# Feed-forward input transposed by VectorE and transfers instead of TensorE, for seven of twelve chunks

## The reference

```
x = x + attn_a(layernorm(x), Wq, bq, Wk, bk, Wv, bv, Wo, bo)     # 16 heads of 16, softmax over 512 keys
x = x + ffn(layernorm(x), W1, W2, W3)
x = x + attn_b(layernorm(x), Wv, Wg, bg, Wq, bq, Wo)             # sigmoid gates, decaying scan over the sequence
x = x + ffn(layernorm(x), W1, W2, W3)

def ffn(x, W1, W2, W3):          # D = 256, H = 1024
    hidden = silu(x @ W1.T) * (x @ W3.T)
    hidden = fwht(hidden)        # Walsh-Hadamard transform, folded into W2 here
    return hidden @ W2.T
```

## Time and profile before

| what | value |
|---|---|
| median of 3 runs | 574.08 us (574.04 to 577.14) |
| the profiled execution | 574.17 us, its span 572.4 us |
| busy share of TensorE, VectorE, ScalarE, GpSimd | 97%, 65%, 56%, 31% |
| moved by transfers | 25.74 MB in 17979 packets |

### The profile page before, as it was taken

How to read it: one execution, slowest core, us unless ns; L and a number is a source line. 1 busy time by engine, 2 the same in 40 slices (tenths; PEclk the granted TensorE clock), 3 DMA queues, 4 the chain that set the end, 5 groups by cost and what they waited for, 6 DMA issues and landing times.

```text
span 572.4 us, 8932 instructions
## 1 busy us (share of the span) xinstructions
PE 557.8 (97%) x3276; PEld 388.6 (68%) x3276; DVE 374.2 (65%) x715; ACT 319.7 (56%) x595; POOL 176.4 (31%) x209
## 2 busy tenths in 40 slices
PE   8999999999999988899999999999999999999997
PEld 4543433344334433378888888888888888988887
DVE  6998878888888899754363544747886336254433
ACT  3678888867876886833234242266775333434231
POOL 5796375552545333510101010223332010101000
PEclk9999999999999999999999999999999999999999
DMA  7357320330032020010000000000000010010101
GB/s 230 101 185 236 118 74 3 113 112 2 18 124 86 25 125 3 12 64 1 1 0 1 1 1 2 1 0 1 1 1 1 2 37 1 1 37 1 38 1 38
DMA packets 17979, 25.74 MB, mean 45 GB/s; under 512 B 3032, under 2 KB 11224, under 8 KB 17552
## 3 DMA queue, kind: packets, MB, share of 16 engines
q1 hardware_dynamic: 16716, 24.10, 13.0%
q10 hardware_dynamic: 1220, 1.07, 0.6%
HBM read 10.89 MB, written 5.24 MB: 28 GB/s over the span
## 4 chain that ended last, share of the span: by engine, by line
PE 89%; DVE 4%; ACT 3%; issue 2%; DMA 1%; ACTq 0%; POOL 0%; SPq 0%; DVEq 0%; POOLq 0%
PE PS L367 86%; DVE mxr L1077 3%; PE PS L378 2%; ACT qf L805 1%; ACT PR L912 1%; PE PS L585 1%; DMA X<-in_x 1%; DVE PR L1216 0%; DVE OT L1142 0%; DMA ring<-mT 0%; ACT XNs L974 0%; ACT XNs L965 0%; ACTq L874 0%; DVE X L1244 0%; ACT xf L789 0%
## 5 line engine op out<-in xcount | busy, mean ns | idle before, releaser
L367 PE MATMUL PS<-xTh,ring 128*128 128x512 f32 x608 | 188.7, 392 | 0.0
L1077 DVE TENSOR_REDUCE mxr<-PS 128x1 f32<-128x512 f32 x256 | 163.1, 682 | 26.4 <-PE PS L367 25.8
L912 ACT ACTIVATE PR<-PS 128x512 f32<-128x512 f32 x256 | 138.2, 604 | 35.9 <-PE PS L367 35.5
L367 PEld LDWEIGHTS PS<-xTh,ring 128*128 128x128 f32 x608 | 113.2, 188 | 23.6 <-issue 1.7
L367 PE MATMUL PS<-xTl,ring 128*128 128x512 f32 x304 | 110.1, 391 | 0.0
L367 PE MATMUL PS<-ring 50*128 50x512 f32 (+1 forms) x512 | 99.3, 450 | 5.0 <-DVE mxr L1077 3.8
L1216 DVE TENSOR_TENSOR PR<-PR,PS 128x512 f32<-128x512 f32 x64 | 43.8, 684 | 88.7 <-PE PS L367 66.4
L789 ACT ACTIVATE AOh<-PR 128x512 fp32r<-128x512 f32 x72 | 45.5, 632 | 95.5 <-DVE PR L1216 89.6
L367 PEld LDWEIGHTS PS<-ring 50*128 50x128 f32 (+1 forms) x512 | 41.3, 184 | 82.4 <-ACT PR L912 54.9
L1319 POOL TENSOR_TENSOR xTl<-xf,xTh 128x512 fp32r<-128x512 f32 x30 | 41.1, 1384 | 144.4 <-ACT xTh L789 144.4
L980 ACT ACTIVATE PR<-PS 128x512 f32<-128x512 f32 x64 | 38.0, 594 | 79.2 <-PE PS L367 79.2
(11 more groups left out here) (132 smaller groups left out, 635.1 us busy)
## 6 DMA issues: line engine op xcount, KB each, us to landing
ring<-qh SPq DMA_DIRECT2D x48, 128.0 KB, 2.7
ring<-ql SPq DMA_DIRECT2D x24, 128.0 KB, 2.7
ring<-weight_scratch SPq DMA_DIRECT2D x3, 1024.0 KB, 4.8
weight_scratch<-in_w SPq DMA_DIRECT2D x2, 1024.0 KB, 6.7
X<-in_x SPq DMA_DIRECT2D x3, 512.0 KB, 6.7
out<-X SPq DMA_DIRECT2D x6, 256.0 KB, 2.2
X<-in_w SPq DMA_DIRECT2D x1, 1024.0 KB, 5.4
ring<-AOh SPq DMA_DIRECT2D x8, 128.0 KB, 2.8
```

The costliest lines, as they stand in the source:

```text
L367: return nc.tensor.matmul(dst, lhsT, rhs, start=start, stop=stop, skip_group_check=True)
L912: nc.scalar.activation(PR[:, j % 8, :], PS[:, kq_bank(j), :], ACT.Exp, scale=HD ** -0.5)\
L1077: nc.vector.tensor_reduce(mxr[:, S % 2, blk, TT * p + t:TT * p + t + 1], PS[:, QK0 + i % 3, :], AX.X, ALU.max, negate=True).then_inc(max_d ...
```

## The change

For the seven preparations named above, TensorE's transposes and ScalarE's copies out of the banks go. In their place:

- `normalise` writes `XNs` in another order, (half of the features, token tile, feature), so that each half is a stretch of 512 columns. It comes after f = 1 and not after f = 3, and `prepare` after f = 0 and not f = 1.
- `turn_blocks`, after f = 2, VectorE: two `transpose` of 128 by 512 from `XNs` to `PR` slots 4 and 5. Each turns the 32 by 32 blocks in themselves; a block stays on its 32 partitions.
- `turned_blocks`, SP: 16 transfers, one for each pair of a source and a destination group of 32 partitions, from `PR` to `xf`. Each moves 32 partitions by 8 runs of 32 float32 values (128 bytes), 32 KB in 256 runs. SP waits for `lnT_ready` (the two transposes) and `x_lo` (`xf` free again) ahead of them.
- ScalarE: no `ln_evacuate`; `ln_hi` comes after f = 6 and not f = 5 and waits until all 16 transfers have landed (`xf_in`).
- In chunk 3, `centre` stays after f = 5, `scale` comes behind `ln_hi` after f = 6, and the two extra statistics come after f = 3 and f = 4.

```diff
+        def by_dim(v):
+            return v.rearrange("p t n -> p (t n)").rearrange("p (k t u) -> p k t u", k=KD, u=P)
+        def turned_block(a, c):
+            u = slice(32 * a, 32 * a + 32), slice(32 * c, 32 * c + 32)
+            return (xf[u[1], :, :].rearrange("p k (t u) -> p (k t) u", u=P)[:, :, u[0]],
+                    PR[u[0], 4:6, :].rearrange("p k (t u) -> p (k t) u", u=P)[:, :, u[1]])
...
+            def turned_blocks(L):
+                sp.wait_ge(lnT_ready, 2 * L + 2)
+                sp.wait_ge(x_lo, 2 * L)
+                for a in range(4):
+                    for c in range(4):
+                        sp.dma_start(*turned_block(a, c)).then_inc(xf_in, DMA)
             weights_in(W_MEM)
+            for n in range(BATCH):
+                turned_blocks(n + BATCH + 1)
...
+                if c < BATCH - 1:
+                    turned_blocks(3 * BATCH + 1 + c)
...
-                    if f == 4 and not last:
-                        pe.wait_ge(xns_ready, n + BATCH + 1)
-                        if n == 0:
-                            pe.wait_ge(x_done, 2 * BATCH)
-                        ln_transpose(0, PS[:, 6, :])
-                        ln_transpose(1, PS[:, 7, :])
...
-                    pe.wait_ge(x_f, 2 * (n + BATCH + 1))
+                    pe.wait_ge(x_f, 2 * (n + 1))
...
             def ln_hi(L, dt, par):
-                act.wait_ge(x_f, 2 * (L - 1) + dt + 1)
+                n = L - BATCH - 1
+                if n % (2 * BATCH) < BATCH and n >= 0:
+                    act.wait_ge(xf_in, 16 * DMA * (n + 1 - n // (2 * BATCH) * BATCH))
+                else:
+                    act.wait_ge(x_f, 2 * (L - 1) + dt + 1 - (2 * BATCH if n >= 0 else 0))
...
-                    if n == BATCH - 1 and f == 6:
-                        scale(1, 0)
-                    if f == 5 and not last:
+                    if n == BATCH - 1 and f == 5:
+                        centre(2 * BATCH + 1, 1, 0)
+                    if f == 6 and not last:
                         for dt in range(KD):
-                            ln_evacuate(n + BATCH + 1, dt, PS[:, 6 + dt, :])
                             ln_hi(n + BATCH + 1, dt, 1 - par)
                         if n == BATCH - 1:
-                            centre(2 * BATCH + 1, 1, 0)
+                            scale(1, 0)
...
+            def turn_blocks(L, i):
+                dve.wait_ge(xns_ready, L)
+                if i:
+                    dve.wait_ge(xf_in, 16 * DMA * i)
+                for dt in range(KD):
+                    nc.vector.transpose(PR[:, 4 + dt, :], by_dim(XNs[:, :, :])[:, dt, :, :].rearrange("p t u -> p (t u)"))\
+                        .then_inc(lnT_ready, 1)
...
-                    if f == 1 and not last and not prepared:
+                    if f == 0 and not last and not prepared:
                         dve.wait_ge(x_done, 2 * (n + BATCH) - 2 * (n == 0))
                         pause()
                         prepare(n, X0)
-                    if n == BATCH - 1 and f in (2, 4):
-                        pause()
-                        prepare(BATCH + f // 2 - 1, f // 2 * TT, f // 2 * TT)
-                    if f == 3 and not last:
+                    if f == 1 and not last:
                         dve.wait_ge(rstd_done, n + 6)
                         normalise(X0, X0 if prepared else 0, n + BATCH + 1)
+                    if f == 2 and not last:
+                        turn_blocks(n + BATCH + 1, n - n // (2 * BATCH) * BATCH)
+                    if n == BATCH - 1 and f in (3, 4):
+                        pause()
+                        prepare(BATCH + f - 3, (f - 2) * TT, (f - 2) * TT)
...
+            dve.wait_ge(xf_in, 16 * DMA * BATCH)
             for c in range(BATCH):
                 mem_chunk(BATCH + c, TT * c, TT * ((c + 3) % BATCH))
```

More of the change, by code:

```diff
@@ L145, in build @@
             sem(n) for n in ("swhi_done", "swlo_done", "rwhi_done", "rwlo_done", "stk_ready", "stk_tmp", "stk_done"))
+        xf_in = sem("xf_in")
         nmean_done, nmem_done, mem_centred = (sem(n) for n in ("nmean_done", "nmem_done", "mem_centred"))
@@ L1061, in normalise @@
             def normalise(X0, n0, L):
-                if L:
-                    dve.wait_ge(lnT_ready, 2 * L)
+                dve.wait_ge(lnT_ready, 2 * L)
                 for t in range(TT):
-                    last = normalise_tile(X0 + t, n0 + t, t)
+                    last = nc.vector.tensor_scalar(by_dim(XNs[:, :, :])[:, :, t, :],
+                                                   X[:, X0 + t, :].rearrange("p (k u) -> p k u", k=KD),
+                                                   mom[:, n0 + t:n0 + t + 1, 0], rstd[:, n0 + t:n0 + t + 1],
+                                                   ALU.subtract, ALU.mult)
                 last.then_inc(xns_ready, 1)
+            def turn_blocks(L, i):
[5 more added lines that the diff above has]
+                        .then_inc(lnT_ready, 1)
             def lo(dst, src, h):
```

## The result

The changed kernel takes 567.52 us (median of 4 executions, 567.37 to 567.80) against 574.17 (574.04 to 577.14) beside it: 1.16% less by the medians, ratio 0.9873 [0.9844, 0.9902]. The forecast was 568.1, so the direction held and the gain was larger than forecast: 6.65 us by the medians, where 6.1 were summed. At those the kernel before takes 574.1 and the changed one 567.35 (median of six in a second series), 6.8 apart.

The account below looks back on a forecast made before the run. TensorE, busy 97% of the span, was taken as the bound. 574.17 less 6.1 for the transposes of seven chunks, plus 0 for the added work, gave 568.1 us; the range was 567.4 to 578.0.

Parts of the forecast that it names:

- worth nothing by themselves: ScalarE's 14 copies out of the banks: ScalarE has room, so removing them was counted as no gain.
- TensorE's transposes, 0.87 us in each of seven chunks: TensorE's stream in the feed-forward chunks: eight transposes removed save 0.87 us a chunk, 6.1 us in seven.
- VectorE's two transposes and the moves, at nothing: VectorE: two transposes of 704 ns per chunk and moved statistics and normalisation cost nothing, as products keep room.
- Rival 3: VectorE's statistics and transposes push a product past TensorE's need, about 0.3 us a chunk; 569 to 570; chance 0.05.
- Issue decides and the fixed part overlaps: SP's transfers: issue at 0.55 to 0.62 us each sets the pace, not packets; the fixed part is not paid serially.
- The rule of the Trainium skill against transfers under 64 KB: Weighed against the 16 transfers: were about 2.0 us paid serially, a set takes 32 us, losing about 129 us.
- The landing, 10.2 to 11.2 us: Time from VectorE's transposes until all 16 transfers of a set have landed, at 0.55 to 0.62 us each.
- the rooms: Time the transfers have before TensorE waits at `down(7)`: 13.7 us in chunk 1, 12.8 in chunk 0, 12.6 in chunk 3.
- Rival 1: Transfers land a little late through slower issue or packets; total 568.7 to 571, say 569.9; chance 0.15.
- Rival 2: 128-byte runs are expensive; ScalarE waits at `ln_hi`, TensorE stops at `down(7)` in seven chunks; up to 613; chance 0.16.
- A wait of about 0.3 at `down(7)` as before: Chunk 3: TensorE's existing 0.32 us wait at `down(7)` was to stay at about 0.3 us.
- a handoff more saved in each chunk: Reason for the range's low end, 567.4: one further handoff saved in every chunk.

Follow-up runs that it names:

- copies_gone: pe_gone without ScalarE's 14 copies out of the banks as well, the layer's input left out; 567.66 us, ratio 0.989.
- pe_gone: Kernel before without TensorE's 56 transposes in the seven chunks, nothing in their place, ScalarE's copies kept; 568.3 us, ratio 0.9909.
- order_only: Kernel before with only VectorE's new order of statistics and normalisation, transposes and copies kept; 574.07 us, ratio 0.9992.
- extra6: Changed kernel with six transfers more in each of the seven sets, 22 in all, ScalarE waiting for them too; 588.33 us, ratio 1.0207.
- runs1k: Changed kernel with each transfer's 32 KB in 32 runs of 1 KB, the transposition left out; 567.38 us, ratio 0.9857.
- runs64: Changed kernel with each transfer's 32 KB in 512 runs of 64 bytes, the transposition left out; 567.83 us, ratio 0.9873.

## Why the prediction was right, and where it missed

The forecast of 568.1 was 0.6 us over the 567.52 measured, and 0.75 over the 567.35 at full clock. The step that failed is the work of ScalarE in chunk 3, put at nothing twice: its copies were "worth nothing by themselves", and the stall at `down(7)` was to stay "as before". copies_gone shows that the copies made that stall, and that they are worth 0.57 us.

**TensorE's transposes, 0.87 us in each of seven chunks:** right, to the hundredth. The chunks of 34.27 us fell to 33.40, and pe_gone shows the part alone.

**VectorE's two transposes and the moves, at nothing:** right. 686 ns for 704 taken, 1.38 us for the normalisation, and order_only is within 0.1 us of before; with the transposes added too, no wait of TensorE for a product is listed. Rival 3 is out.

**Issue decides and the fixed part overlaps:** right. The sum of all landings one after the other would be 16 x 1.9 = 30 us in a set; measured are 11.7 to 13.1. The rule of the Trainium skill against transfers under 64 KB (DMA: Bandwidth & Descriptors, rules for kernel authors), which the prediction weighed, does not bite here, since the landings lie beside each other and the issues are hidden; extra6 shows how near it is, with 22 transfers slower than the kernel before. The 2.0 us that the prediction took from that page of the Trainium skill are given there for transfers issued by GpSimd; these are issued by SP, and the trace has 1.9. The read-modify-write for transfers under 512 bytes, of which the specifications on that page of the Trainium skill speak, is not seen in the time to landing: with runs of 64 bytes it is 2.0 us for 1.9. The section of the same Trainium skill page on small descriptors says that transfers between SBUF and SBUF don't suffer the penalty of short ones. The time to landing agrees; the engines' time does not, as the same 32 KB take 0.20 us of 16 engines in 128-byte runs and 0.13 in runs of 1 KB. What that difference is made of, no run here shows.

**The landing, 10.2 to 11.2 us:** too low; it was 11.7 (chunk 0) to 13.1 (chunk 1), 0.5 to 1.9 over the upper value. The distance of issues is 0.65 us, not 0.55 to 0.62; landing took 1.9 us, not 1.8; and the set of chunk 1 took 11.74 us where that of chunk 0 took 10.42, the longest issue of the span being 1952 ns for a median of 611. It cost next to nothing, because the rooms were right: 12.7, 13.5 and 14.3 us in chunks 3, 0 and 1, where 12.6, 12.8 and 13.7 were forecast. Rival 1 came about only in its mildest form, 0.21 us in chunk 3 of one of the two profiled executions. The margin was thinner than forecast: 12.6 less 10.2 to 11.2 leaves 1.4 us and more in chunk 3, and nothing of it was left, so that the gain is kept there by luck as much as by the reckoning. Two issues more make a loss of 1.4 us.

**Rival 2:** excluded by the packet's 11.9 ns, where 53 would have been needed for over 1%. Its mechanism is real all the same, and extra6 shows it: ScalarE at `ln_hi` with silu of tile 7 behind it, TensorE stopped at `down(7)`. Its price can be more than the length of the stalls, as the clock behind two of them shows.

**"A wait of about 0.3 at `down(7)` as before", and the copies "worth nothing by themselves":** this is the step that failed. It has two errors. First, the size: the bracket in the earlier trace rows says 0.32, but the chunk was 34.85 - 34.27 = 0.58 us longer than its neighbours. TensorE's matmuls overlap, and the bracket counts only from the modelled end of the last one; the four stalls measured here are 0.31, 0.95, 1.40 and 0.32 by bracket and 0.63, 1.28, 1.66 and 0.58 by the chunk's length, 0.26 to 0.33 more each time. Second, the sign: I had ScalarE's copies "worth nothing by themselves", while ScalarE in chunk 3 has no idle time from the rounding of tile 5 to silu of tile 6, so that their time (0.58 us each) stood in front of everything up to `down(7)`. Their removal, copies_gone, is worth 0.57 of the 0.63 us that the stall costs in pe_gone. I had looked for what the new order adds in that chunk and not for what it takes away. In the changed kernel 0.21 came back in one profiled execution and nothing in the other; in the first `xTh` began 0.22 us later behind the rounding of tile 6 (0.78 for 0.56), and the issues of the set, 11.56 us long there and 11.33 in the second, fit that.

**The sum.** 6.09 (the transposes) + 0.58 (the stall of chunk 3) + 0.11 (chunk 7) = 6.8 us, against 6.8 at full clock (574.1 to 567.35). The 0.11 is in the last memory chunk (12.09 to 11.98), and its cause is open. None of the parts that were tried alone brings it: without the transposes, with VectorE's or ScalarE's new order and without the copies, the chunk has 12.07 or 12.09. What the rows show of it is on VectorE, of pe_gone and of the changed kernel:

```profile
424.70 0.69 DVE L1263 SCALAR_TENSOR_TENSOR PR<-PS,PR 128x512 f32<-128x512 f32 x1 [0.67 <-PE PS L367]
...
427.52 1.24 DVE L1273 SCALAR_TENSOR_TENSOR PR<-PR 128x512 f32<-128x512 f32 x1 [0.39 <-ACT PR L999]
```

```profile
424.35 0.69 DVE L1297 SCALAR_TENSOR_TENSOR PR<-PS,PR 128x512 f32<-128x512 f32 x1 [0.31 <-PE PS L390]
...
427.52 0.89 DVE L1307 SCALAR_TENSOR_TENSOR PR<-PR 128x512 f32<-128x512 f32 x1 [0.75 <-ACT PR L1020]
```

With TensorE and ScalarE at the same places, VectorE starts 0.35 us earlier, and a multiplication that begins at the same time takes 0.89 and not 1.24. GpSimd's `xTl` runs beside both, from 426.40 on, for 3.17 and 3.52 us. Whether they hinder each other was not tried, and why VectorE starts earlier is not known.

**The range.** Its low end, 567.4, allowed "a handoff more saved in each chunk" and nothing for the stall. 567.52 lies just inside; the ratio of 0.9873 on 574.08 is 566.8 and lies below it. That ratio is of the means of four executions each, and the 577.14 of the kernel before is one of them; without it the means give 0.9885, or 567.5. The stall alone, gone, puts the time at 574.17 - 6.1 - 0.6 = 567.5, so the low end had to lie below that.

## What to carry to other kernels

Work that is taken off an engine with room elsewhere can still be worth time in the one stage in which that engine has no idle time: look for the chunk that is longer than its neighbours, and go by the pitch of the chunks, since the bracket of a stall on TensorE read about 0.3 us too little here. A way through VectorE and many small transfers took 0.65 us for each issue and 1.9 once at the end, and may be had for nothing if so much time lies between the source and the first reader; what it needs then is a count of that room before anything else, since six issues more in each set turned a gain of 1.2% into a loss of 2.1%, the lower clock behind the stalls included.

## What the runs showed of the hardware that was not expected

- An issue on SP took 0.59 us with 32 runs in it, 0.61 with 256 and 0.63 with 512 (medians). A transfer of 32 KB between SBUF and SBUF took 0.13, 0.20 and 0.31 us of the 16 engines with them (runs1k, the changed kernel, runs64); a packet of 128 bytes was 11.9 ns of one engine's time.
- The longest issue of each kernel took 1.6 to 2.0 us, about three times the median. Its cause was not looked into.
- In extra6 the granted clock was 0.50 for about 7 us from the end of an idle time of 3.09 us on TensorE on, and for about 3.5 us behind one of 3.39 us; behind the four of 2.00 us and less it stayed at 1.00. The second does not show in the page's slices of 14.7 us.
